# Attention's score maxima: read over units of two PSUM banks, with one maximum per query block, in place of single-bank tiles

## The reference, cut to what matters

```python
x = L0_attn_query
x = x + 0.5 * _L0_ffn_ref(_layernorm(x), ...)      # stage A
x = x + _L0_attn_ref(_layernorm(x), ...)           # stages A (projections), B, C (output projection)
x = x + 0.5 * _L0_ffn_ref(_layernorm(x), ...)      # stage C

# inside the attention, 16 heads of 16 features, all in f32
scores = jnp.einsum('bhqd,bhkd->bhqk', q, k)
scores = jnp.where(causal[None, None], scores, -jnp.inf)
attn = jax.nn.softmax(scores, axis=-1)
out = jnp.einsum('bhqk,bhkd->bhqd', attn, v)
```

## Time and profile before

| | |
|---|---|
| Median of 3 runs | 1353.83 us (1350.99 to 1354.71) |
| The profiled execution's own time | 1353.6 us |
| Its span in the trace | 1351.8 us |
| Stage B in the span | about 306 to 1148 us |
| Busy over the span | PE 92%, DVE 84%, ACT 68%, GpSimd 32% |
| TensorE clock granted, mean | 0.963 of full speed |

### The profile page before, as it was taken

One profiled execution on the slowest core, in us unless ns is written; L12 is line 12 of the kernel. 1 busy time (PEld: TensorE's weight loads), 2 busy tenths in 40 slices (PEclk: granted clock), 3 DMA queues, 4 the chain that ended last, 5 costly groups with the idle time before them and its releaser, 6 DMA issues. The chain is left out here.

```text
span 1351.8 us, 37753 instructions
## 1 busy us (share of the span) xinstructions
PE 1245.0 (92%) x9324; PEld 825.8 (61%) x9324; DVE 1138.3 (84%) x4510; ACT 920.7 (68%) x1858; POOL 435.0 (32%) x843
## 2 busy tenths in 40 slices
PE   4999999978999999999999999999999997699996
PEld 3988888964554454554554554554554543599996
DVE  4788888749999999999999999999999994367775
ACT  3666666630777777777777777777777777356654
POOL 3333333301222222222222222222322322467772
PEclk9999999985899999999999999999999999699998
DMA  3366666881564564664664664664664663556651
GB/s 113 141 225 225 225 225 225 220 274 37 78 107 81 99 106 80 101 104 80 103 102 80 103 102 80 104 101 80 106 99 80 106 99 107 158 180 196 192 165 63
DMA packets 121900, 174.12 MB, mean 129 GB/s; under 512 B 44012, under 2 KB 71788, under 8 KB 121804
## 3 DMA queue, kind: packets, MB, share of 16 engines
q1 hardware_dynamic: 121816, 173.30, 56.4%
HBM read 96.08 MB, written 76.02 MB: 127 GB/s over the span
## 5 line engine op out<-in xcount | busy, mean ns | idle before, releaser
L1000 ACT ACTIVATE b_probs<-bank 128x512 f32<-128x512 f32 x1152 | 597.4, 612 | 135.4 <-PE bank L1124 131.6
L1027 DVE CUSTOM_DVE_ANT_0 b_junk<-bank,mask 128x512 bf16<-128x512 f32 (+3 forms) x1032 | 446.8, 488 | 1.4 <-issue 1.2
L1030 DVE TENSOR_REDUCE b_pm<-bank 128x1 f32<-128x512 f32 x516 | 322.4, 683 | 19.7 <-PE bank L1101 18.7
L1143 PE MATMUL bank<-b_probs,b_vx 128*32 128x512 f32 (+3 forms) x3072 | 310.3, 499 | 4.2 <-ACT b_o L985 1.9
L1124 PE MATMUL bank<-qs,ks 50*128 50x512 f32 (+3 forms) x1056 | 293.6, 383 | 4.3 <-ACT b_probs L1000 0.4
L1101 PE MATMUL bank<-ks,qs 48*128 48x512 f32 (+3 forms) x1056 | 277.2, 390 | 10.9 <-PEq L443 6.3
L1101 PEld LDWEIGHTS bank<-ks,qs 48*128 48x128 f32 x1056 | 165.1, 193 | 134.6 <-DVE b_pm L1030 61.5
L145 POOL TENSOR_TENSOR hold_pool<-zero 128x1 f32<-128x1 f32 x192 | 37.4, 195 | 629.9 <-ACT b_probs L1000 474.3
L1124 PEld LDWEIGHTS bank<-qs,ks 50*128 50x128 f32 x1056 | 159.7, 188 | 57.3 <-ACT b_probs L1000 52.4
L960 POOL TENSOR_SCALAR_AFFINE_SELECT b_probs<-b_probs 128x512 f32<-128x512 f32 x256 | 158.5, 638 | 0.0
L1143 PEld LDWEIGHTS bank<-b_probs,b_vx 128*32 128x32 f32 x3072 | 71.1, 109 | 109.6 <-issue 80.9
(11 more groups left out here) (120 smaller groups left out, 1993.8 us busy)
## 6 DMA issues: line engine op xcount, KB each, us to landing
scr_qk<-a_qk SPq DMA_DIRECT2D x64, 512.0 KB, 3.2
qs<-scr_qk SPq DMA_DIRECT2D x132, 128.0 KB, 4.5
ks<-scr_qk SPq DMA_DIRECT2D x132, 128.0 KB, 5.1
scr_o<-b_o SPq DMA_DIRECT2D x64, 256.0 KB, 3.7
b_qs<-scr_qk SPq DMA_DIRECT2D x66, 128.0 KB, 4.0
b_ks<-scr_qk SPq DMA_DIRECT2D x66, 128.0 KB, 4.6
a_x<-x SPq DMA_DIRECT2D x16, 512.0 KB, 3.5
scr_x<-a_x SPq DMA_DIRECT2D x16, 512.0 KB, 2.7
```

Source lines behind the costliest of these rows:

```text
L1000: act.activation(probs[:, PROB_BUF[s], h, :], score_bank(g, t, last)[:], ACT.Exp).then_inc(p_ready, 1)
L1027: ins = dve.tensor_tensor_reduce(junk[:, t % MB, off:off + w], src, mask[:, BANK - w:BANK], 1.0, 0.0, ALU.add, ALU.max, pm[:, g.buf, 0, pl ...
L1030: ins = dve.tensor_reduce(pm[:, g.buf, 1, place(h), i:i + 1], src, AX.X, ALU.max)
L1143: last = pe.matmul(o_bank[2 * D * h:2 * D * (h + 1), col:col + w], vx[g.buf][:, j, h, :], probs[:, PROB_BUF[src], h, off:off + w], start=( ...
```

## The change: what it does

The table `MAX_SLOTS` is replaced by `UNITS`: 18 units in a group, each a pair of adjacent banks (1024 columns) that one or two whole query blocks of one head or two fill. Blocks 5 and 1, 4 and 2, 6 and 0 share a unit for each head, block 7 has one by itself, and two blocks 3 of different heads share one. DVE waits once for both tiles of a unit and reads each query block with one custom instruction of 128 to 1024 columns, across the two banks. TENSOR_REDUCE and the joining step are gone, and `part` has two steps. PE waits at a unit's first tile only, until the unit two before it is read. PE's order in a round becomes M0 S0 M1 S1 M2 S2 V M3 S3, with the max tiles one place further ahead (13 are issued ahead of the first score tile in place of 12), the order of heads in the score tiles changes, and the PSUM banks are allocated in pairs. The matmuls of the max tiles stay 48 in a group.

```diff
-S_ORDER, M_ORDER = (1, 3, 0, 2), (0, 2, 1, 3)
+S_ORDER = (1, 0, 2, 3)
-MAX_SLOTS = [
-    [(3, 0, 512, 0)],
...
-    [(6, 512, 384, 0), (4, 512, 128, 384)],
-    [(1, 0, 256, 0), (5, 512, 256, 256)],
-]
+def unit_of(*tiles):
+
+    pieces, reads, at = [[], []], [], 0
+    for i, h in tiles:
+        reads.append((i, h, at, (i + 1) * P))
+        for k0 in range(0, (i + 1) * P, BANK):
+            w = min(BANK, (i + 1) * P - k0)
+            pieces[at // BANK].append((i, h, k0, w, at % BANK))
+            at += w
+    assert at == 2 * BANK and all(sum(p[3] for p in bank) == BANK for bank in pieces)
+    return pieces, reads
+
+UNITS = ([unit_of((5, h), (1, h)) for h in range(GH)] + [unit_of((4, h), (2, h)) for h in range(GH)] +
+         [unit_of((6, h), (0, h)) for h in range(GH)] + [unit_of((3, s), (3, s + 2)) for s in range(2)] +
+         [unit_of((7, h)) for h in range(GH)])
+UNITS = UNITS[:12] + UNITS[14:] + UNITS[12:14]
+NUNIT = len(UNITS)
+UNITS_AHEAD = AHEAD * GH // 2
...
-            def maximum(g, a, n):
...
+            def maximum(g, u):
+
+                pieces, reads = UNITS[u]
+                dve.wait_ge(m_tile, g.at(TILES, 2 * u + 2))
+                if not (g.first and u < 2):
+                    dve.wait_ge(m_read, g.at(NUNIT, u - 1))
+                hold.dve(dve, u % 4)
+                for i, h, off, w in reads:
+                    src = m_pair[u % 2][:, off:off + w]
+                    ins = dve.tensor_tensor_reduce(junk[:, u % 2, off:off + w], src, mask[:, 2 * BANK - w:2 * BANK], 1.0, 0.0,
+                                                   ALU.add, ALU.max, pm[:, g.buf, place(h), i:i + 1])
                 ins.then_inc(m_read, 1)
...
             def next_maxima(g):
-                for a in range(AHEAD):
-                    for h in range(GH):
-                        if a == 0 and h < 3:
-                            part(g, h)
-                        maximum(g.next(1), a, h)
+                for u in range(UNITS_AHEAD):
+                    if u < 2:
+                        part(g, u)
+                    maximum(g.next(1), u)
...
-                if not (g.first and t < MB):
-                    pe.wait_ge(m_read, g.at(TILES, t - MB + 1))
-                for i, k0, w, off in MAX_SLOTS[a]:
+                if t % 2 == 0 and not (g.first and u < 2):
+                    pe.wait_ge(m_read, g.at(NUNIT, u - 1))
+                for i, h, k0, w, off in UNITS[u][0][t % 2]:
...
                 for s in range(NSLOT):
-                    score_tile(g, s, 0, last)
-                    maxima(s, 0)
-                    score_tile(g, s, 1, last)
-                    maxima(s, 1)
-                    maxima(s, 2)
-                    score_tile(g, s, 2, last)
-                    event(g, s)
-                    if s == TURN_SLOT and not last:
-                        turn_m(g.next(1))
-                    maxima(s, 3)
-                    score_tile(g, s, 3, last)
+                    for n in range(GH):
+                        maxima(s, n)
+                        score_tile(g, s, n, last)
+                        if n == GH - 2:
+                            event(g, s)
+                            if s == TURN_SLOT and not last:
+                                turn_m(g.next(1))
```

More of the change, by code:

```diff
@@ L86 @@
 PROB_BUF[LOW_DONE] = 3
-MAX_SLOTS = [
[9 rows of a table removed]
-]
+def unit_of(*tiles):
[13 more added lines that the diff above has]
+NUNIT = len(UNITS)
+assert NUNIT % 2 == 0 and all(t[1] % 2 == u % 2 for u in range(NUNIT) for t in UNITS[u][1])
 EARLY = (B - 1) * H
 SB, MB = 3, 4
+UNITS_AHEAD = AHEAD * GH // 2
 TURN_SLOT = NSLOT - AHEAD
@@ L385, in __init__ @@
         self.ks = [ar.sb(f"ks{n}", [P, PAIRS, T], F32R) for n in range(self.GROUPS)]
-        self.mask = ar.sb("mask", [P, BANK])
+        self.mask = ar.sb("mask", [P, 2 * BANK])
         self.stacked = [ar.sem(f"stacked{n}") for n in range(NBUF)]
@@ L403, in pool_mask @@
         chain(pool.memset(self.mask[:], 0.0))
-        diag = self.mask[:, BANK - P:BANK]
+        diag = self.mask[:, 2 * BANK - P:2 * BANK]
         chain(pool.affine_select(out=diag, in_=diag, compare_op=ALU.is_ge, fill=MASKED, base=0,
@@ L768, in _, with stage_b @@
             qkv(NCHUNK - 1, range(QKV), last=True)
-def stage_b(nc, psum, const, scratch, ahead, chunk):
+def stage_b(nc, psum, pairs_of_banks, const, scratch, ahead, chunk):
     ident, _, zero, *_, hold = const
@@ L1035, in part @@
                 if n == 0:
[L1036 to L1044, removed]
+                    dve.wait_ge(m_read, g.at(NUNIT, NUNIT))
+                    if not g.first:
+                        dve.wait_ge(m_turned, g.at(1))
                 if n == 1:
+                    dve.wait_ge(m_chain, g.at(2, 1))
+                whole = pm[:, g.buf, :, :].rearrange("p (s g) i -> p s (g i)", s=2)
+                if n == 0:
                     ins = dve.tensor_scalar(mparts[:, 0:2, 0, :], whole, -1.0, None, ALU.mult)
@@ L1068, in step @@
                     return
-                for a in range(AHEAD, NSLOT):
-                    for h in range(GH):
-                        maximum(g.next(1), a, h)
+                for u in range(UNITS_AHEAD, NUNIT):
+                    maximum(g.next(1), u)
                 next_maxima(g.next(1))
-            for a in range(NSLOT):
-                for h in range(GH):
-                    maximum(Group(0, 0), a, h)
+            for u in range(NUNIT):
+                maximum(Group(0, 0), u)
             next_maxima(Group(0, 0))
@@ L1082, in turn_m @@
             def turn_m(g):
[L1084 removed]
+                pe.wait_ge(m_chain, g.at(2, 2))
                 if g.k or not isinstance(g.r, int):
@@ L1601, in macaron @@
         ar = Arena(nc, ctx)
-        psum = [ctx.enter_context(nc.psum_tensor(f"bank{n}", [P, BANK], F32)) for n in range(8)]
+        pairs_of_banks = [ctx.enter_context(nc.psum_tensor(f"banks{n}", [P, 2 * BANK], F32)) for n in range(4)]
+        psum = [pairs_of_banks[n // 2][:, n % 2 * BANK:(n % 2 + 1) * BANK] for n in range(8)]
         ident = ar.sb("ident", [P, P])
@@ L1613, in macaron @@
             stage_a(nc, psum, const, io, scratch, ahead)
-            stage_b(nc, psum, const, scratch, ahead, chunk)
+            stage_b(nc, psum, pairs_of_banks, const, scratch, ahead, chunk)
         stage_c(nc, psum, const, io, scratch, chunk)
```

33 lines of the change are left out of this document (15 added, 18 removed), and 6 rows, old and new, of the table MAX_SLOTS.

## The result

The changed kernel took 1333.05 us (median of 4 runs, 1330.34 to 1335.07) against 1352.41 for the kernel before, run beside it (median of 4, 1349.7 to 1354.71): a ratio of 0.9856, 95% interval 0.9826 to 0.9886, 19.4 us less. Measured again it was 1329.55 against 1352.64, ratio 0.9831 (0.9807 to 0.9855). The forecast was 1327 with a range of 1311 to 1341.

The account below looks back on a forecast made before the run. The prediction took a cycle through PE and ACT, not DVE, as the bound in stage B. Gains of 24.8 + 1.5 + 0.5 = 26.8 us gave 1327 us from a median of 1353.83, range 1311 to 1341.

Parts of the forecast that it names:

- What bounds the kernel: Stage B: PE and ACT wait on each other in a cycle that sets the pace; DVE only follows.
- Ordinary rounds: Stage B rounds without the transpose or a V of another width: 2.64 us each, unchanged by cheaper DVE reads.
- that rival: DVE sets the pace, so its saved time all comes back: period 23.8 us, gain 46 us, 1307 us; chance 0.06.
- The steps of `part`: Sixth round of each group: the last step comes earlier, the transpose's 0.80 us stall goes, gaining 24.8 us.
- The cover of M1: PE's wait at M1 for a whole unit, 0.15 to 0.2 us, is hidden by ACT's work on S3: cost 0.
- The round with the short V: Round with a V of 256 columns: PE waits less for DVE, 0.05 us a group, 1.5 us in all.
- The start: First group's maxima, DVE's alone: 1.2 us less reading against a thirteenth tile ahead; gain taken as 0.5 us.
- The signs: Period 24.4 to 24.5 us, transpose round 2.9, transpose 1.0 behind V, ACT's rounds 2.64 apart, DVE about 90% busy.
- DVE's reads: Wide reads across two banks cost no extra: 1.15 us for 1024 columns, 21.8 us a group against 23.0 before.
- the slower case: Waits for whole units bind at M1: at 1.45 us a unit, 37 us slower, 1390 us; chance 0.07.
- a ring: Stage B's cycle through PE and ACT: S3's exponential, S2, V, new S3; 0.65 + 0.42 + 1.00 + 0.57 = 2.64 us.

Follow-up runs that it names:

- the old reads: Kernel before, with all three steps on the maxima ahead of tile 0 of the next group, reads and banks unchanged: 1329.44 us, ratio 0.9837.
- Scores first: Changed kernel with the old order in a round, S0 M0 S1 M1 M2 S2 V M3 S3: 1324.67 us, ratio 0.9824; again 1328.97 us, ratio 0.9835.
- V in halves: Changed kernel with the value step V cut in two, half behind S2 and half behind S3: 1507.86 us, ratio 1.1142.
- a fourth score bank: Kernel before with steps on the maxima at tiles 0, 0, 1, and PSUM banks divided 4 for scores, 3 for maxima: 1411.6 us, ratio 1.0438.
- the late step: Changed kernel with the last step on the maxima one unit later, ahead of unit 2 in place of unit 1: 1382.37 us, ratio 1.0213.
- 256 columns: Changed kernel with a memset of 256 columns ahead of each unit's reads on DVE: 1396.33 us, ratio 1.0338.
- A memset of 64 columns: Changed kernel with a 64-column memset ahead of each unit's reads on DVE: 1336.76 us, ratio 0.9888.

## Why the prediction was right, and where it was off

- **What bounds the kernel: right.** Ordinary rounds stayed 2.64 us while DVE's work fell, and stayed 2.64 with DVE 97% busy under the old reads. The Trainium skill, Perfetto Trace Analysis, "Identifying the Most-Contended Engine", would have DVE optimised first, as the engine of highest occupancy. Here that is DVE (95%, PE's weight loads 50%, which I had put at 49); the trace doesn't agree, and the 1307 us of that rival did not come about.
- **The steps of `part`: right in place and size.** The round fell by 0.81 us in the group shown and by 0.79 in the mean of 30 (predicted 0.80), the margin was 0.28 us (predicted 0.3), the new round 2.90 (predicted 2.91). 31 * 0.79 = 24.5 us against 24.8. Moving the steps alone gives the whole effect, moving one back turns it into a loss.
- **The cover of M1: the term that was mis-sized.** I took 0, "covered by ACT's work on S3". The wait was larger than I said (0.37 and 0.41 us against 0.15 to 0.2). In most rounds the cover held, but in two M1 was late enough to make S2 late, 0.05 and 0.09 us in the group shown, 0.04 and 0.11 in the mean: 0.15 * 31 = 4.7 us. Scores first, in which S0 and S1 don't stand behind the waiting tile, gives 0.12 of it back. I had compared M1 with S2's due time by mean distances (with S2 due 1.22 us behind M3 by the earlier trace rows, not 1.24); one has to add up each round by itself.
- **The round with the short V:** 0.02 us (2.50 to 2.48) in place of 0.05: 0.6 us in place of 1.5.
- **The start:** I took a gain of 0.5 us. From stage B's first matmul to the copy at 358.7 it was a loss of 1.3 (53.4 us against 52.1; 53.5 when run again), of which the earlier start of stage B hid 1.0. The first group's maxima, from DVE's first read to the first step of `part`, took 23.6 us against 23.0 (306.68 to 330.30, 307.25 to 330.26): no gain from cheaper reads. The units of two reads take 1.23 us and 1.38 to 1.50 us there in turn (309.31, 310.54, 312.03 are three starts), with PE at its lower clock (0.50 from 305.3 to 332.4). I take the longer ones for waits for whole units; which part the thirteenth tile has was not tried.
- **Sum:** 24.5 - 4.7 + 0.6 - 0.3 = 20.1 by the mean rounds, 19.8 by the periods and the start, 19.4 by the medians, against 26.8. The misses all point the same way: no error hid another, and the range was met because the largest term was right.
- **The signs:** the transpose's round, its 1.0 us behind V and ACT's ordinary rounds came as named. The period was 24.61, not 24.4 to 24.5, and DVE's busy share 94%, not about 90%: its busy time fell by 1.0 us a group (24.13 to 23.14), not by 1.5.
- **DVE's reads: right.** The two-bank read had no extra price (1.16 us for 1024 columns, predicted 1.15), and a unit took 1.24. Had it cost a tenth more, all would have been lost: the chance of only 0.07 for the slower case rested on this one straight line.

## What to carry to other kernels

An engine can be 95% busy and still be the follower; before you make its work cheaper, look in the timeline for the one place where something else waits for it, and ask whether only the order there must change. Here moving small steps past one or two tiles gave as much time as a rewrite of the tiles, reads and banks (1329.44 and 1329.55 us). When you have found a ring, use it to price waits in it, but not to price another order: both attempts to shorten it (V in halves, a fourth score bank) made the kernel slower.

## What I had not expected of the hardware

- A DVE read across two PSUM banks follows the line of single-bank reads: 768 columns 0.88 us from start to start, 1024 columns 1.16, against 0.62 for 512.
- TensorE's granted clock fell below its full level inside stage B in four experiments: to 0.61 in the stretch shown of the late step, to 0.79 over 100 us with V in halves, to a mean of 0.97 over 700 us with three max banks, and to 0.99 with 256 columns. In the kernel before and the changed one it was 1.00 from 400 to 1090 us. PE was busy less in all four (651, 627, 631 and 618 us from 400 to 1100, against 669 before), but the least busy lost the least, so busy time alone doesn't tell. What brings the clock down stays open; these losses lie on top of the stalls' own.
- A memset of 64 columns, its own row 112 ns long, made a unit longer by 0.06 us only; part of it lies beside the read before.
